# Reciprocals spread by fp16 matmuls, two steps moved to GpSimd, a third context piece, and new orders in a gated cross-attention block

## Chip, cores and metric

The kernel runs on one core of a Trainium2 chip. The metric is the device time of one execution in microseconds (us); lower is better. Of three runs the kernel before took 1135.02 us in the median (1132.27 to 1136.66).

## What is computed

x is 16 batches of 224 rows and 512 columns, the context 16 batches of 750 keys and 384 columns, with a mask over the keys; 8 heads of 64; the FFN has 2048 hidden columns.

```python
q = (layernorm(x) @ W_q);  k = context @ W_k;  v = context @ W_v      # split into 8 heads of 64
sim = einsum('bihd,bjhd->bhij', q, k) * 64 ** -0.5;  sim = where(mask, sim, -max)
x = x + tanh(g_xattn) * (softmax(sim) @ v @ W_o + b_o)
# bitlinear: rmsnorm the input, round it to 8 bits by its row's largest value; weights rounded to -1, 0, 1 by their mean
h = gelu(bitlinear(layernorm(x), w1, b1))
x = x + tanh(g_ffn) * bitlinear(h, w2, b2)
```

## The kernel before

Attention goes by batches: 16, each with two halves of 112 rows, 8 heads in 4 pairs, and so 16 score tiles of 112x750 (numbers u). The FFN goes by 28 tiles of 128 rows. Nearly every fp32 operand of the attention is split into an fp16 high part and an fp16 rest, and each product is three matmuls (high with high, rest with high, high with rest).

The order of the work is written out by hand as a list of steps, each named (kind, number), with a batch: START for the first batches, SLOTS for one round of a loop in which each step has a stage (which batch it works on relative to the round), and END. Every engine walks the same list and emits only its own part of a step, so the list fixes each engine's order; what engines wait for is said by semaphores (`need`). SP's queue (all loads, stores and transposes), GpSimd's and VectorE's are strictly in order.

The steps that matter here, with lines of the profile:

- LC loads one of three context pieces of a batch into one of two places (L482, it waits until GpSimd has used the piece two before). CX splits it: ScalarE makes the fp16 high part (L931), GpSimd the rest (L995). K and V need all three.
- LX loads x. N1 takes mean and variance on VectorE (L736, L740), and GpSimd raises the variance to the power -1/2 (L1008, L1011). XN subtracts the mean from x in place on VectorE (L744). XH scales and splits it (L925, L748), XT transposes it (L490), Q projects it.
- S makes two heads' scores of a half on TensorE (L574). M adds the mask and takes the row minimum on VectorE (L701), E exponentiates on ScalarE with a row sum (L881), H makes the fp16 high part on ScalarE (L888) or GpSimd (L979), L the rest on GpSimd (L984), T transposes both through SP (L507). There are five places for scores in SBUF, and M waits until L has freed one.
- R takes reciprocals of two row sums on VectorE (L708), 8 steps a batch. PV on TensorE first spreads the reciprocals of four (head, half) pairs over partitions by matmuls with the fp32 identity (L585, 112x64 stationary, 112 columns moving, fp32), then sums V weighted by the probabilities (L597, 36 matmuls of 224 columns). The two heads of a pair go side by side into the two halves of the array's columns. ScalarE copies the spread reciprocals out (L893) and VectorE multiplies (L713, step PA); PL splits the result (L899, L990).
- O is the output projection of a tile. L2 takes its statistics, subtracts the mean and finds the largest value, L3 derives the scale (L780 to L787), L4 multiplies and adds a large constant that rounds to an integer (L792) and subtracts it again (L797), both on VectorE. XQ transposes it, F1 is the first FFN product (L633), GE the gelu (L937), GS its sum of squares (L944), GM its largest value (L814), G2 the power and the scale (GpSimd L1038, L1041, then VectorE L821 to L828), GI the multiplication that rounds (GpSimd L1047), G3 the subtraction of the constant (VectorE L835), HT the transpose (L525), F2 the second product (L641) and the store.
- Weights are loaded and split once at the start (PD, PW), and the FFN's weights are rounded among the first two batches (WL, WA, WM, WB, WR, WQ).

## Time and profile before

| | |
|---|---|
| median of 3 runs | 1135.02 us |
| profiled execution | 1132.84 us |
| its span, first to last instruction | 1131.0 us |
| mean granted TensorE clock | 0.98 |
| busy: TensorE, VectorE, ScalarE, GpSimd | 91%, 80%, 70%, 76% |
| TensorE's weight loads (beside its matmuls) | 54% |

The profile is of one execution. A busy share is an average over stages with different limits, so the stretch has to be looked at. TensorE runs in pairs and pipelined: the time that a group occupies is read from the start of one group to the start of the next, rather than from its own busy time. "Waited for" names the engine and line whose work came last before an instruction could start.

### The profile page before, as it was taken

Reading aid. Unit: us, or ns where it says so; the run is one execution under the profiler, and the core shown is the slowest. Engines: PE = TensorE matmul, PEld = TensorE weight load, DVE = VectorE, ACT = ScalarE, POOL = GpSimd, SP = SyncE. Lnnn points to the kernel's source line nnn. Section 1 sums busy time; section 2 is a strip of 40 time slices with the busy share of each in tenths; the row PEclk is TensorE's granted clock in tenths of the full one; section 3 lists DMA queues with packets and bytes.
Section 4 is the critical chain, followed back from the end, with each engine's and each line's share of the span. In section 5 each row is a group of like instructions: output and inputs, shape, how many; then the busy total and the mean of one; then the engine's idle time right before and its main releaser. Section 6 shows DMA issues by size and latency. Waiting matters only on the chain.

```text
span 1131.0 us, 23832 instructions
## 1 busy us (share of the span) xinstructions
PE 1033.3 (91%) x8372; PEld 610.6 (54%) x8372; DVE 909.8 (80%) x1768; ACT 794.7 (70%) x1389; POOL 862.6 (76%) x767
## 2 busy tenths in 40 slices
PE   3869999999999899999999899999999999999575
PEld 2436556565555555565565555555565555655332
DVE  4678787979899587979989677998989778787764
ACT  4989685876868576786858668585967759586522
POOL 3389977787977778797877868788786879867832
PEclk9979999999999999999999999999999999999878
DMA  8778969777777977879687777868676896766822
GB/s 258 256 188 157 198 108 176 136 166 143 152 161 126 194 130 129 148 154 181 119 179 132 154 149 138 173 120 182 128 157 133 154 185 106 138 132 131 141 61 65
DMA packets 480005, 170.77 MB, mean 151 GB/s; under 512 B 458256, under 2 KB 460048, under 8 KB 479504
## 3 DMA queue, kind: packets, MB, share of 16 engines
q1 hardware_dynamic: 479888, 169.25, 74.6%
q8 instruction: 68, 1.11, 0.4%
q14 instruction: 49, 0.40, 0.1%
HBM read 48.09 MB, written 7.34 MB: 49 GB/s over the span
## 4 chain that ended last, share of the span: by engine, by line
PE 55%; POOL 16%; DVE 10%; issue 8%; DMA 6%; ACT 4%; SPq 1%; DVEq 0%; ACTq 0%; POOLq 0%
PE ps_g L544 29%; POOL p L984 8%; PE ps_g L641 7%; PE ps_g L597 6%; PE ps_s L574 6%; PE ps_g L633 5%; DMA hqt<-hq 4%; POOL p L979 2%; PE ps_g L585 2%; DVE prob L701 2%; DVE hq L835 1%; DVE xa L744 1%; ACT prob L881 1%; DMA xt<-xh 1%; POOL h_sb L1047 1%
## 5 line engine op out<-in xcount | busy, mean ns | idle before, releaser
L984 POOL TENSOR_TENSOR p<-prob,p 112x750 f16<-112x750 f32 x256 | 416.4, 1638 | 9.0 <-ACT p L888 4.9
L701 DVE CUSTOM_DVE_ANT_0 prob<-ps_s,mbias 112x750 f32<-112x750 f32 x256 | 235.6, 930 | 55.8 <-PE ps_s L574 52.9
L881 ACT ACTIVATE prob<-prob,rmin 112x750 f32<-112x750 f32 x256 | 233.6, 913 | 26.1 <-DVE rmin L701 25.8
L544 PE MATMUL ps_g<-ctx,wk 128*128 128x375 f16 x1152 | 203.2, 327 | 19.8 <-POOL ctx L995 18.1
L544 PE MATMUL ps_g<-wv,ctx 128*128 128x512 f16 (+1 forms) x864 | 204.0, 382 | 9.2 <-POOL ctx L995 6.2
L574 PE MATMUL ps_s<-k_sb,q_sb 64*112 64x375 f16 x1536 | 150.2, 328 | 17.0 <-DVE rmin L701 16.7
L544 PEld LDWEIGHTS ps_g<-ctx,wk 128*128 128x128 f16 x1152 | 108.3, 98 | 105.3 <-issue 35.5
L544 PEld LDWEIGHTS ps_g<-wv,ctx 128*128 128x128 f16 (+1 forms) x864 | 88.5, 104 | 96.5 <-issue 9.3
L888 ACT ACTIVATE p<-prob 112x750 f16<-112x750 f32 x160 | 129.5, 819 | 5.5 <-DMA pt<-p 4.6
L574 PEld LDWEIGHTS ps_s<-k_sb,q_sb 64*112 64x112 f16 x1536 | 90.5, 127 | 74.6 <-issue 41.9
L979 POOL CAST p<-prob 112x750 f16<-112x750 f32 x96 | 104.2, 1086 | 28.1 <-ACT prob L881 27.9
L641 PE MATMUL ps_g<-w,hqt 128*128 128x512 fp8e4 x432 | 100.5, 387 | 24.1 <-DMA hqt<-hq 24.1
L597 PE MATMUL ps_g<-pt,v_sb 128*64 128x224 f16 x2304 | 121.6, 259 | 0.2 <-DMA pt<-p 0.2
L597 PEld LDWEIGHTS ps_g<-pt,v_sb 128*64 128x64 f16 x2304 | 112.0, 110 | 0.4 <-issue 0.4
L633 PE MATMUL ps_g<-w,xqt 128*128 128x512 fp8e4 x432 | 102.0, 389 | 5.8 <-DMA xqt<-xq 5.6
L905 ACT ACTIVATE k_sb<-ps_g 128x375 f16<-128x375 f32 x128 | 61.1, 478 | 57.7 <-PE ps_g L544 56.9
L919 ACT ACTIVATE v_sb<-ps_g 128x512 f16<-128x512 f32 x96 | 56.5, 590 | 50.8 <-PE ps_g L544 50.8
L544 PE MATMUL ps_g<-xt,wq 128*128 128x224 f16 x768 | 85.5, 262 | 5.8 <-DMA xt<-xh 5.4
L893 ACT ACTIVATE rb<-ps_g 128x224 f32<-128x224 f32 x64 | 22.5, 351 | 92.5 <-PE ps_g L597 92.5
L995 POOL TENSOR_TENSOR ctx<-ctx_f,ctx 128x750 f16<-128x750 f32 x48 | 75.2, 1568 | 15.7 <-ACT ctx L931 14.8
L1047 POOL TENSOR_SCALAR h_sb<-h_sb,smh 128x2048 f32<-128x2048 f32 x27 | 53.3, 1974 | 41.3 <-DVE smh L828 41.3
L641 PEld LDWEIGHTS ps_g<-w,hqt 128*128 128x128 bf16 x432 | 42.1, 99 | 76.2 <-issue 30.6
(131 smaller groups left out, 1675.1 us busy)
## 6 DMA issues: line engine op xcount, KB each, us to landing
ctx_f<-in_ctx SPq DMA_DIRECT2D x48, 375.0 KB, 3.9
xa<-in_x SPq DMA_DIRECT2D x16, 448.0 KB, 4.8
xr<-in_x SPq DMA_DIRECT2D x28, 256.0 KB, 3.5
out<-xr SPq DMA_DIRECT2D x28, 256.0 KB, 2.3
pt<-p SPq DMA_TRANSPOSE x256, 3.9
h_sb<-in_w SPq DMA_DIRECT2D x4, 512.0 KB, 5.9
xr<-in_w SPq DMA_DIRECT2D x4, 512.0 KB, 6.7
pt<-in_w SPq DMA_DIRECT2D x3, 512.0 KB, 9.4
```

The source lines that it names most:

```text
L544: mm = nc.tensor.matmul(out, lhs, rhs, start=(m == 0), stop=(m == len(steps) - 1))
L574: mm = nc.tensor.matmul(ps_s[0:HT, e, c, 0:CH], q_sb[rows, j, qa, half * HT:(half + 1) * HT], k_sb[rows, j, ka, c * CH:(c + 1) * CH], star ...
L597: mm = nc.tensor.matmul(g[e * DH:(e + 1) * DH, 0:TQ] .rearrange("p (a q) -> p a q", a=2), v_sb[:, p, t, va, (2 * n + e) * DH:(2 * n + e + ...
L633: mm = nc.tensor.matmul(g[:, :], xqt_t[:, k, :], w1v[:, k, f * 512:(f + 1) * 512], start=(k == 0), stop=(k == KD - 1))
L641: mm = nc.tensor.matmul(g[:, :], hqt_t[:, k, :], w2v[:, k, :], start=(k == 0), stop=(k == KF - 1))
L701: nc.vector.tensor_tensor_reduce(prob[:, (b * NU + n) % PROBS, :].rearrange("p (c k) -> p c k", c=2), ps_s[0:HT, n % 2, :, 0:CH], mbias[:, ...
L881: nc.scalar.activation(prob[:, (b * NU + n) % PROBS, :], prob[:, (b * NU + n) % PROBS, :], ACT.Exp, bias=rmin[:, n:n + 1], scale=-1.0, acc ...
L888: nc.scalar.activation(p16[:, u % HILO, 0, 0:J], prob[:, (b * NU + n) % PROBS, :], ACT.Copy)\
L979: nc.gpsimd.tensor_copy(p16[:, u % HILO, 0, 0:J], prob[:, (b * NU + n) % PROBS, :]).then_inc(hi_pool, 1)
L984: nc.gpsimd.tensor_tensor(p16[:, u % HILO, 1, 0:J], prob[:, (b * NU + n) % PROBS, :], p16[:, u % HILO, 0, 0:J], ALU.subtract).then_inc(s[" ...
L995: nc.gpsimd.tensor_tensor(ctx[:, 1, n, :], ctx_f[:, (b * KC + n) % 2, :], ctx[:, 0, n, :], ALU.subtract)\
L1047: nc.gpsimd.tensor_scalar(h_t[:, :], h_t[:, :], smh[:, t % 2, 6:7], MAGIC, ALU.mult, ALU.add).then_inc(s["h_int"], 1)
```

## The change

1. **Reciprocals.** R now handles four at a time (4 steps a batch): after the reciprocal, VectorE makes an fp16 high part scaled by 1024 and, in a third instruction, the fp16 rest. Each waits for the one before. The identity is fp16 and holds 1/1024. PV spreads both parts with two accumulating fp16 matmuls in place of one fp32 matmul.
2. **Third context piece.** The third piece of the first batch has a place of its own (in the buffer of the transposed probabilities, not yet in use), so its load and that of the first piece of the next batch wait for less.
3. **XN** goes to GpSimd, as x times 1 plus the negated mean, after one small instruction that negates the means.
4. **The first half of L4** (multiply and add the constant) goes to GpSimd in the same form; VectorE then waits for it before the second half.
5. **Orders.** START, SLOTS, END and some stages are new. TensorE's order in the loop is nearly the same. At the start SP's queue was LC0, PD0, LC1, LM0, LX0, PD1, LC2 and becomes LC0, LC1, LX0, LM0, PD0, LC2, PD1; GpSimd's was MB, CX0, CX1, N1, CX2 and becomes N1, XN, CX0, CX1, MB, CX2; ScalarE's was PW0, CX0, CX1, XH0, XH1, CX2 and becomes CX0, XH0, XH1, CX1, CX2, PW0. For the last two tiles GpSimd's order was G2, GI, G2, GI and becomes G2, G2, GI, GI.

```diff
+RS = 1024.0
...
-        ident = sb("ident", [128, 128], F32)
+        ident = sb("ident", [128, 128], F16)
...
+        nm1 = sb("nm1", [HT, 2], F32)
...
+        rr16 = sb("rr16", [HT, 2, NU], F16)
...
+        def ctx_place(c):
+            return pt_words[:, 3 * WCH:3 * WCH + J] if c == KC - 1 else ctx_f[:, c % 2, :]
+
         def need_ctx(eng, c):
-            eng.wait_ge(d_ctx[c % 2], 16 * (c // 2 + 1))
+            if c == KC - 1:
+                eng.wait_ge(d_ctx[2], 16)
+            else:
+                eng.wait_ge(d_ctx[c % 2], 16 * (c // 2 + 1 - (c >= KC and c % 2 == 0)))
...
                     c = b * KC + n
-                    need(sp, "ctx_lo", 0, c - 2)
-                    sp.dma_start(ctx_f[:, c % 2, :], ctx_d[b, :, n, :]).then_inc(d_ctx[c % 2], 16)
+                    if c >= KC:
+                        need(sp, "ctx_lo", 0, c - 2 if c > KC + 1 else 1)
+                    sp.dma_start(ctx_place(c), ctx_d[b, :, n, :]).then_inc(d_ctx[2 if c == KC - 1 else c % 2], 16)
...
-                    need(pe, "recips", b, 2 * n + 1)
+                    need(pe, "recips", b, n)
                     for m in range(2 * n, 2 * n + 2):
                         at = 256 + half_of(b, m) * HT
-                        for e in range(2):
-                            nc.tensor.matmul(g[e * DH:(e + 1) * DH, at:at + HT],
-                                             rrec[:, 2 * m + e:2 * m + e + 1].to_broadcast([HT, DH]),
-                                             ident[0:HT, 0:HT], start=True, stop=True)
+                        for a in range(2):
+                            for e in range(2):
+                                nc.tensor.matmul(g[e * DH:(e + 1) * DH, at:at + HT],
+                                                 rr16[:, a, 2 * m + e:2 * m + e + 1].to_broadcast([HT, DH]),
+                                                 ident[0:HT, 0:HT], start=(a == 0), stop=(a == 1))
...
                 elif kind == "R":
-                    need(dve, "expd", b, 2 * n + 1)
-                    need(dve, "weighted", b - 1, n // 2)
-                    nc.vector.reciprocal(rrec[:, 2 * n:2 * n + 2], rsum[:, 2 * n:2 * n + 2])\
-                        .then_inc(s["recips"], 1)
+                    of = slice(4 * n, 4 * n + 4)
+                    need(dve, "expd", b, 4 * n + 3)
+                    need(dve, "weighted", b - 1, n)
+                    nc.vector.reciprocal(rrec[:, of], rsum[:, of]).then_inc(s["recips_f"], 1)
+                    need(dve, "recips_f", b, n)
+                    nc.vector.tensor_scalar(rr16[:, 0, of], rrec[:, of], RS, None, ALU.mult).then_inc(s["recips_hi"], 1)
+                    need(dve, "recips_hi", b, n)
+                    nc.vector.scalar_tensor_tensor(out=rr16[:, 1, of], in0=rrec[:, of], scalar=RS, in1=rr16[:, 0, of],
+                                                   op0=ALU.mult, op1=ALU.subtract).then_inc(s["recips"], 1)
...
-                elif kind == "XN":
-                    for half in range(2):
-                        need(dve, "x_mean", b, half)
-                        nc.vector.tensor_scalar(xa[:, half, :], xa[:, half, :], mv1[:, half, 0:1], None,
-                                                ALU.subtract).then_inc(s["x_cent"], 1)
...
-                    need_tile(dve, "x2_mult", t)
-                    nc.vector.tensor_scalar(xc[:, :], xc[:, :], sm2[:, t % 2, 6:7], MAGIC, ALU.mult, ALU.add)\
-                        .then_inc(s["x2_int"], 1)
...
+                elif kind == "XN":
+                    need(pool, "x_mean", b, 1)
+                    need(pool, "x_cent", b - 1, 1)
+                    nc.gpsimd.tensor_scalar(nm1[:, :], mv1[:, :, 0], -1.0, 0.0, ALU.mult, ALU.add)\
+                        .then_inc(s["x_less"], 1)
+                    need(pool, "x_less", b, 0)
+                    for half in range(2):
+                        nc.gpsimd.tensor_scalar(xa[:, half, :], xa[:, half, :], 1.0, nm1[:, half:half + 1],
+                                                ALU.mult, ALU.add).then_inc(s["x_cent"], 1)
+                elif kind == "L4":
+                    t = tile_of(b, n)
+                    need_tile(pool, "x2_mult", t)
+                    nc.gpsimd.tensor_scalar(xc[:, :], xc[:, :], sm2[:, t % 2, 6:7], MAGIC, ALU.mult, ALU.add)\
+                        .then_inc(s["x2_int"], 1)
```

The last line of END, with the old order of GI:0 and G2:1 (and F2:1 of batch 14) above and the new one below:

```diff
-    GM:1:-1 G3:0:-1 GI:0:-1 G2:1:-1 G3:1:-1 F2:0:-1 GI:1:-1 F2:1:-1
+    F1:4:-1 F1:5:-1 F1:6:-1 F1:7:-1 GM:0:-1 G2:0:-1 HT:0:-1 HT:1:-1 GS:1:-1 F2:1:-2 GM:1:-1 G2:1:-1 GI:0:-1 G3:0:-1
+    G3:1:-1 F2:0:-1 GI:1:-1 F2:1:-1
```

## Rows read from the trace of the kernel before

**Rows 1.** The page, part 1: busy us, share of the span, instructions.

```profile
PE 1033.3 (91%) x8372; PEld 610.6 (54%) x8372; DVE 909.8 (80%) x1768; ACT 794.7 (70%) x1389; POOL 862.6 (76%) x767
```

**Rows 2.** Busy us by stretch, with instruction counts, granted clock, DMA share and GB/s.

```profile
0.00:84.00 84.00, 51.81 (x310) 29.12 (x310) 52.06 (x94) 63.55 (x106) 45.37 (x44) 0.92 0.77 236
...
150.00:575.00 425.00, 415.11 (x3431) 247.38 (x3425) 361.34 (x710) 315.01 (x555) 346.79 (x307) 1.00 0.78 149
575.00:1000.00 425.00, 409.36 (x3355) 243.69 (x3357) 357.11 (x697) 302.62 (x534) 333.60 (x295) 1.00 0.76 147
```

**Rows 3.** TensorE's waits (us, times, longest): 150 to 1000, then 1000 to 1131.

```profile
PE ps_g L641 <- DMA hqt<-hq: 11.1, 7, 2.1
...
PE ps_s L574 <- DVE rmin L701: 10.3, 3, 5.8
```

**Rows 4.** Timeline of TensorE, 503 to 520: start, duration, line, operation, tiles, count.

```profile
503.50 0.60 PE L585 MATMUL ps_g<-ident,rrec 112*64 112x112 f32 x8
503.93 1.90 PE L597 MATMUL ps_g<-pt,v_sb 128*64 128x224 f16 x36
505.76 1.32 PE L544 MATMUL ps_g<-xt,wq 128*128 128x224 f16 x12
...
516.62 3.04 PE L544 MATMUL ps_g<-ctx,wk 128*128 128x375 f16 x18
519.49 0.81 PE L544 MATMUL ps_g<-wv,ctx 128*128 128x512 f16 x3
```

**Rows 5.** Groups by line and shape: count | busy us, mean ns | idle before.

```profile
L984 POOL TENSOR_TENSOR p<-prob,p 112x750 f16<-112x750 f32 x256 | 416.4, 1638 | 9.0 <-ACT p L888 4.9
...
L1047 POOL TENSOR_SCALAR h_sb<-h_sb,smh 128x2048 f32<-128x2048 f32 x27 | 53.3, 1974 | 41.3 <-DVE smh L828 41.3
...
L744 DVE TENSOR_SCALAR xa<-xa,mv 112x512 f32<-112x512 f32 x32 | 42.5, 1368 | 0.0
...
L792 DVE TENSOR_SCALAR xc<-xc,sm 128x512 f32<-128x512 f32 x28 | 30.8, 1098 | 0.1
...
L708 DVE RECIPROCAL rrec<-rsum 112x2 f32<-112x2 f32 x128 | 19.8, 156 | 23.4 <-ACT prob L881 23.2 <-issue 0.2
...
L770 DVE TENSOR_SCALAR xc<-xr,mv 128x512 f32<-128x512 f32 x28 | 14.1, 504 | 1.0
L1002 POOL TENSOR_SCALAR mbias<-mask 112x750 f32<-112x750 uint8 x16 | 13.8, 862 | 6.4 <-DMA mask<-in_mask 5.1
```

**Rows 6.** Timeline of all engines, 9 to 19.

```profile
10.61 1.29 DVE L736 BATCH_NORM_STATS2 st<-xa 112x6 f32<-112x512 f32 x2 [1.65 <-DMA xa<-in_x]
11.36 0.35 SPq L482 DMA_DIRECT2D ctx_f<-in_ctx  x1
...
12.98 0.25 POOL L1008 TENSOR_SCALAR ve<-mv 112x2 f32<-112x2 f32 x1
...
16.38 1.60 POOL L995 TENSOR_TENSOR ctx<-ctx_f,ctx 128x750 f16<-128x750 f32 x1 [2.23 <-ACT ctx L931]
...
18.14 1.10 PE L544 MATMUL ps_g<-ctx,wk 128*128 128x375 f16 x3 [18.14 <-POOL ctx L995]
```

**Rows 7.** Timeline of all engines, 1109 to 1124.

```profile
1110.11 1.97 POOL L1047 TENSOR_SCALAR h_sb<-h_sb,smh 128x2048 f32<-128x2048 f32 x1 [1.49 <-DVE smh L828]
...
1113.38 0.19 POOL L1038 TENSOR_SCALAR smh<-smh 128x1 f32<-128x1 f32 x1 [1.30 <-ACT k_sb L944]
1113.50 1.22 DVE L835 TENSOR_SCALAR hq<-h_sb 128x2048 bf16<-128x2048 f32 x1
1113.65 1.47 POOL L1041 TENSOR_TENSOR smh<-smh,half_neg 128x1 f32<-128x1 f32 x1
1114.74 1.96 SPq L525 DMA_TRANSPOSE hqt<-hq  x1
...
1119.13 5.16 PE L641 MATMUL ps_g<-w,hqt 128*128 128x512 fp8e4 x16 [9.28 <-DMA hqt<-hq]
```

## What the change should do to the time

> **What bounds the kernel now.** I read the share of busy time first, and stretch by stretch rather than as one average. TensorE is busy for 1033.3 of 1131.0 us [rows 1]. In the middle, from 150 to 1000 us, it is busy for 415.11 + 409.36 = 824.5 of 850 us [rows 2], so 25.5 us of idle time are left in 850, at a granted clock of 1.00, the 2.4 GHz level. In the same 850 us VectorE works 718.5 us (85%) and GpSimd 680.4 us (80%) [rows 2]. TensorE's largest single wait there is for the transposed FFN input, 11.1 us in seven places [rows 3]. So in the middle a TensorE microsecond taken away is nearly a microsecond of span, and work on the other engines counts only where it makes TensorE late. The rest of TensorE's idle time lies at the ends: 32.2 us in the first 84 us [rows 2], of which the first matmul's start is 18.14 us [rows 6], and the chain behind the last attention product.
>
> **The spread of the reciprocals (TensorE).** Each of the 64 PV steps begins with eight fp32 matmuls (L585: 4 products, each recorded as two) that spread the reciprocals over partitions. One such group starts at 503.50 and the weighted sum behind it at 503.93: 0.43 us of TensorE's time, though the row says 0.60, since the ends of matmuls overlap the next ones [rows 4]. The weighted sum itself, 36 fp16 matmuls of 224 columns in pairs, takes 505.76 - 503.93 = 1.83 us, 0.102 us for a pair [rows 4]. A pair of the fp32 ones takes 0.43 / 4 = 0.107 us with half the columns, 112. An fp32 column here costs as much as two fp16 columns. After the change there are still eight matmuls in four pairs, now fp16 with 112 columns. By columns: K's 18 matmuls of 375 columns take 519.49 - 516.62 = 2.87 us [rows 4], 0.159 us each, so 112 columns are 0.048 us, four pairs 0.19 us, and with about 0.05 us for the change-over 0.24 us. The gain is 0.43 - 0.24 = 0.19 us a group, 64 x 0.19 = **12.2 us**. Ends: nothing gained if a pair keeps its 0.107 us for a reason other than columns; at most 0.43 - 4 x 0.051 = 0.23 us a group, 14.5 us. I take 12.2, since every fp16 group in rows 4 goes by its columns.
>
> **The chain behind them (VectorE).** Before, a PV step needs two reciprocals of 0.156 us each, 128 in all, 19.8 us; after, one reciprocal of four columns, one scaling and one subtraction, each waiting for the one before. The two new ones are bounded by 0.15 and, with the wait, 0.25 us; the nearest row is the reciprocal itself, 0.156 [rows 5]. That is about 0.55 us x 64 = 35 us, 15 us more on VectorE. The PV step waits for the last exponential of the same four either way, and also for its transposes, which come behind a 1.64 us subtraction on GpSimd [rows 5], so the extra 0.3 us lies beside longer work: nothing. If that cover is gone, it is 0.3 x 64 = 19 us at most.
>
> **The mean of x and the scaling of the FFN input go to GpSimd.** VectorE loses 42.5 + 30.8 = 73.3 us [rows 5], and with the 15 above is 58 us lighter (80% to 75%). What I see in these rows is that the same subtraction on 128x512 costs 504 ns at L770, but L744 takes 1368 and L792 1098 ns: they are stretched by something beside them, and that goes too. GpSimd takes over 32 + 28 instructions of 512 columns. Its multiply-then-add takes 1974 ns for 2048 columns and 862 for 750 [rows 5]: 0.857 ns a column and 0.22 us fixed, so 0.66 us for 512. That is 60 x 0.66 = 39.6 us, and 16 negated means at 0.25 to 0.32 us (like the 0.25 of L1008 [rows 6]), 4.5 us: 44 us, 2.8 us for each of 16 batches (one takes about 67 us). GpSimd has 170 us idle in 850 [rows 2], 13 us a batch, so I cost it at nothing for TensorE, except as below. Queued behind the moved scaling on GpSimd are the subtractions that feed the transposes and free the score buffers; queued behind VectorE's second half of it are the next minimum and the evictions of K, V and Q that TensorE needs.
> At this place the Trainium skill speaks against the change: its GPSIMD Engine Reference, section "Engine selection", puts elementwise work on VectorE, with GpSimd about twice as slow for two inputs and near line rate for one. The trace agrees for the two-input subtraction and for one input shows 0.66 against 0.50 us unhindered; by the page as by the rows the moved work is a little longer where it goes.
>
> **Waits that take back part of it.** TensorE stands still in several places of a batch until something other than it comes [rows 3]; what is saved just before such a place only lengthens the wait. The bounds are none of the 12.2 us and half of it, or below nothing if the lighter VectorE shortens the waits (at most the 25.5 us of idle time, I allow 5). I take 2.0 us lost, about a sixth, since the idle time is 3% of the stretch and sits at about two places a batch, and there are four PV steps in one.
>
> **The start.** The first matmul waits until 18.14 us for the third context piece. Its load is issued at 11.36, behind GpSimd's work on the first piece, and its own subtraction on GpSimd runs from 16.38 to 18.0 [rows 6]. After the change it has a place of its own and is sixth in SP's queue without a wait; x comes third and wk fifth instead of second. x, fifth before, was there at 10.61 [rows 6] behind some 2.1 MB; with 1.2 MB ahead it lands at about 7.2 us, wk at 10.6 and the third piece at about 12. Then GpSimd's queue sets it: reciprocal deviation and centring of x until about 11.3, three subtractions of 1.6 and the mask's 0.9 us: 17.0 us. The split of wk (ScalarE 1.5, VectorE 1.8 us behind ScalarE's work on x and the pieces) ends at about the same time. So -1.1 us; bounds -3 and +1.5. The rest of the first 84 us is put in a new order with the same work; I cost it at nothing, bounds -5 and +5.
>
> **The end.** In the new order GpSimd does the root mean square of the last tile (G2) before the rounding multiplication of the last but one (GI), where it was the other way round. The last but one's product starts at 1110.11 and lasts 1.97 us, VectorE rounds at 1113.50 for 1.22 us, SP issues the transpose at 1114.74, and TensorE starts the product at 1119.13 [rows 7]. After, the multiplication stands behind the last tile's sum of squares, which GpSimd gets at 1113.38, and 0.19 us and a power: 1.47 us beside VectorE's rounding [rows 7], some 0.6 without it. So it runs from about 1114.2 to 1116.2, the rounding ends at 1117.5 instead of 1114.72, and the last 12 us come **2.8 us** later (bounds 1.5 and 4). Nothing hides this. The scaling of the two last tiles on GpSimd costs 0.66 for 0.5 us and two hand-overs, but in its new place it is not behind VectorE's read of the second output product: nothing, bounds -0.5 and +1.
>
> **The sum**, against the profiled execution's 1132.84 us: - 12.2 - 1.1 + 2.8 + 2.0 = 1124.3 us. That execution lies 2.2 us below the median of the three runs, 1135.02 (1132.27 to 1136.66); I add half of that and forecast **1125.5 us**.
>
> **The rivals.**
> (a) The fp16 pairs are paced by the instruction or its weight load, not by columns. Rows 4 have 36 matmuls with 36 loads in 1.83 us, 0.051 us for one with its load; if that is a fixed price, eight are 0.41 us and the gain is 0.02 x 64 = 1.3 us: 1132.84 - 1.3 - 1.1 + 2.8 = 1133.2, and 1134.4 with the offset. For it: no row shows an fp16 matmul under 224 columns. Against: each stage's time goes by its columns. If the price were higher for short ones, by 0.08 us each, a group would take 8 x 0.08 = 0.64 us, 0.21 more than now: + 13.4 - 1.1 + 2.8, 1148 us, slower. The 0.051 us of rows 4 speaks against it.
> The Trainium skill, TensorE: Matmul & The Clock Gate, section "Back-to-back issue gap", gives 81 ns for one load and matmul at 128 columns in a sustained stream, which is that higher price. Our row of 0.051 us at 224 columns is already below it.
> (b) Slower: GpSimd becomes late. The place is its queue: a scaling that waits for VectorE's multiplier holds the 1.64 us subtractions behind it, the transposes come late, score buffers are not freed, and TensorE waits in its score step, as it does now near the end of the loop for 10.3 us in three places, longest 5.8 [rows 3]. The price is the part of the added 44 us that comes on the path. It cancels the other terms' 8.5 us at a fifth, and makes the kernel slower by 0.5% from 15 us, a third. With half: 1124.3 + 22 = 1146 us. For it: 80% busy in the middle and 84% after, strictly in order. Against: VectorE's relief on the same chains, and 10 us a batch left idle.
> (c) The new orders, above all before 84 and after 1000 us, cost or give 5 to 10 us by themselves, in either direction: 1115 to 1135.
>
> **How the numbers follow.** The forecast's own mechanism, with a time between 1110 and 1129, has 0.60. Rival (a) has 0.12 as no change, and 0.03 as slower. Rival (b) has 0.13 as slower. Rival (c) has 0.12: 0.05 faster, 0.07 no change. A measurement of this kernel can tell about 0.5% from no change, so faster is below 1129.3, slower above 1140.7. That gives faster 0.65, same 0.19, slower 0.16. The range goes from 1132.84 - 14.5 - 3 - 5 = 1110 to 1140, which takes in (a) without change and small forms of (b), and leaves out half of (b) and the higher price of (a).
>
> **What would show it.** The next start behind the L585 line's successor at 0.24 us instead of 0.43; TensorE's idle time between 150 and 1000 us still about 30 us; GpSimd's busy time at about 907 us and VectorE's at about 850; the first matmul at 17 us; the wait before the last but one product some 12 us instead of 9.3 [rows 7]. The forecast is wrong if a group keeps 0.4 us, or if waits for the minimum (L701) or for transposes grow by over 10 us.

## The result, and the profile after

The changed kernel takes 1174.65 us in the median (1170.51 to 1176.19), the kernel before 1135.77 in runs on the same chip: a ratio of 1.0343, with an interval of 1.0307 to 1.0378. It is 3.4% slower, where 1125.5 us (1110 to 1140) was forecast. The profiled execution took 1175.45 us, its span is 1173.7 us, and the mean granted TensorE clock 0.97 instead of 0.98: TensorE was granted the 1.2 GHz level for 79.7 us of this span, where it was 44.4.

The page's part 1 of the changed kernel (busy us, share of the span, instructions), against [rows 1]:

```profile
PE 1031.4 (88%) x8372; PEld 602.1 (51%) x8372; DVE 953.9 (81%) x1772; ACT 796.3 (68%) x1389; POOL 892.5 (76%) x843
```

TensorE is busy for 2 us less. VectorE was given 73 us of work less, was expected at about 850 us, and has 953.9.

Busy us by stretch of the changed kernel (columns as in [rows 2]: the stretch and its length, then TensorE, its weight loads, VectorE, ScalarE and GpSimd, granted clock, DMA share, GB/s):

```profile
0.00:84.00 84.00, 40.91 (x242) 23.16 (x243) 48.77 (x68) 51.77 (x82) 44.20 (x44) 0.88 0.68 217
...
150.00:575.00 425.00, 398.34 (x3331) 235.14 (x3330) 364.03 (x692) 300.42 (x532) 339.30 (x329) 0.99 0.74 143
575.00:1000.00 425.00, 397.44 (x3297) 233.64 (x3294) 361.13 (x679) 302.54 (x529) 339.96 (x317) 0.99 0.76 146
```

Between 150 and 1000 us TensorE is busy for 795.8 us where it was 824.5 [rows 2]: its idle time has doubled, from 25.5 to 54.2 us in 850. In the first 84 us it does 11 us less work. To find where the span grew, I took the first score matmul (L574 before, L585 after) of each batch:

```
                          before    after
first scores, batch 0       29.6     34.4
first scores, batch 1       99.1    116.4
first scores, batch 15    1013.2   1057.4
end of the span           1131.0   1173.7
```

Of the 42.7 us of span, 17.3 are lost by batch 1 (4.8 of them ahead of batch 0), 26.9 in the next fourteen batches, and 1.5 come back behind batch 15.

What TensorE waited for in the changed kernel, whole span (us in total, times, longest):

```profile
PE ps_s L585 <- DVE rmin L713: 33.7, 16, 9.3
PE ps_g L653 <- DVE att L730: 25.4, 11, 2.7
PE ps_g L555 <- POOL ctx L1004: 23.0, 1, 23.0
PE ps_g L653 <- DMA hqt<-hq: 15.4, 6, 10.0
```

The same waits for VectorE in the kernel before, whole span (its L701 is the minimum, its L713 the step PA):

```profile
PE ps_s L574 <- DVE rmin L701: 16.7, 12, 5.8
PE ps_g L585 <- DVE att L713: 2.0, 1, 2.0
```

The multiplied attention output (L730, step PA) is late in eleven places for 25.4 us, where it was one place and 2.0 us. The wait for the row minimum (L713) has doubled; in the middle, from 150 to 1000 us, it went from 2.3 to 10.4 us. Both are VectorE's, and the minimum does not use the reciprocals at all. So I looked at what stands ahead of them in VectorE's queue.

Groups of the changed kernel by line and shape, columns as in [rows 5]:

```profile
L725 DVE SCALAR_TENSOR_TENSOR rr<-rrec,rr 112x4 f16<-112x4 f32 x64 | 64.6, 1010 | 2.2
...
L723 DVE TENSOR_SCALAR rr<-rrec 112x4 f16<-112x4 f32 x64 | 38.3, 599 | 2.2
...
L1029 POOL TENSOR_SCALAR xa<-xa,nm 112x512 f32<-112x512 f32 x32 | 22.1, 695 | 1.8
L1034 POOL TENSOR_SCALAR xc<-xc,sm 128x512 f32<-128x512 f32 x28 | 19.5, 695 | 0.9
...
L721 DVE RECIPROCAL rrec<-rsum 112x4 f32<-112x4 f32 x64 | 10.7, 167 | 0.0
```

The two small instructions of four columns cost 599 and 1010 ns on average. The reciprocal of the same four columns costs 167. Together R takes 64.6 + 38.3 + 10.7 = 113.6 us of VectorE's time; it took 19.8 before, and 35 were forecast. All 64 of one line at a time (min/median/max in ns, first and last start in us):

```profile
L725 DVE SCALAR_TENSOR_TENSOR rr<-rrec,rr x64: 161/1426/2531, 77.7 to 1111.7; 112x4 f16<-112x4 f32 x64
```

The same instruction takes 0.16 us at least and nine times that in the median. The timeline of all engines shows what it depends on. First at 500 us, then at 511 (start, duration, engine, line):

```profile
499.55 0.81 POOL L988 CAST p<-prob 112x750 f16<-112x750 f32 x1
...
500.01 0.37 DVE L723 TENSOR_SCALAR rr<-rrec 112x4 f16<-112x4 f32 x1
...
500.41 0.16 DVE L725 SCALAR_TENSOR_TENSOR rr<-rrec,rr 112x4 f16<-112x4 f32 x1
```

```profile
511.39 0.80 POOL L988 CAST p<-prob 112x750 f16<-112x750 f32 x1
...
511.54 0.17 DVE L721 RECIPROCAL rrec<-rsum 112x4 f32<-112x4 f32 x1
...
511.74 0.48 DVE L723 TENSOR_SCALAR rr<-rrec 112x4 f16<-112x4 f32 x1
512.16 3.08 POOL L993 TENSOR_TENSOR p<-prob,p 112x750 f16<-112x750 f32 x2
512.26 1.43 DVE L725 SCALAR_TENSOR_TENSOR rr<-rrec,rr 112x4 f16<-112x4 f32 x1
...
513.61 0.93 DVE L713 CUSTOM_DVE_ANT_0 prob<-ps_s,mbias 112x750 f32<-112x750 f32 x1
```

Each time, the end of the small instruction is the end of GpSimd's. The cast ends at 500.36 and the scaling at 500.38; at 511.39 + 0.80 = 512.19 the next cast ends, and the scaling at 512.22. The 3.08 us are two subtractions of half that; the first ends at about 513.7, and so does the rest (L725), at 513.69. The reciprocal at 511.54 runs beside the cast and takes no longer. At 500.41 GpSimd runs nothing, and the rest takes 0.16 us. Sorted by what GpSimd ran when it began, L725 took 161 to 165 ns in the 16 places where GpSimd was idle, and in the median 1521 ns in the 37 places beside a subtraction, ending 18 ns after it. Four times it began 0.09 us behind the start of GpSimd's 0.19 us step of two columns (L1025), and there it took 0.16 us: the price is what the instruction beside it has still to run. L723 beside one of GpSimd's steps with two inputs (45 places, 41 of them subtractions) took 649 ns in the median and ended 25 ns after it.

So these instructions have little work of their own; they stand still until GpSimd's running instruction is over, and the minimum (L713, at 513.61) and all that is queued in VectorE stands behind them. The Trainium skill states such a rule: SBUF — State Buffer, section "Who interferes with whom", says that VectorE and GpSimd share a pair of ports, that a two-input VectorE instruction or one in a two-port mode contends for it, and that whoever comes second is blocked for the whole of the other's instruction. The trace agrees, down to four columns, with the 18 and 25 ns above. Which mode the scaling (L723) runs in, no trace shows.

### The profile page after: what moved, and what is told of

The parts are those of the page before. It is cut to its first block, busy times and chain, and to the rows that moved or that the text cites. A ratio compares the mean times of both kernels' runs of the same rounds, so it can differ in the third digit from the quotient of the medians.

```text
span 1173.7 us, 23867 instructions
## 1 busy us (share of the span) xinstructions
PE 1031.4 (88%) x8372; PEld 602.1 (51%) x8372; DVE 953.9 (81%) x1772; ACT 796.3 (68%) x1389; POOL 892.5 (76%) x843
## 4 chain that ended last, share of the span: by engine, by line
PE 38%; DVE 25%; issue 15%; POOL 9%; DMA 7%; ACT 3%; SPq 1%; DVEq 0%; ACTq 0%; POOLq 0%
PE ps_g L555 18%; DVE prob L713 7%; PE ps_g L653 7%; PE ps_g L645 5%; PE ps_g L609 4%; PE ps_s L585 4%; POOL p L993 3%; DVE hq L844 3%; DMA hqt<-hq 2%; DVE smh L823 2%; DMA pt<-p 2%; DVE rr L723 2%; DVE h_sb L816 1%; DMA xqt<-xq 1%; DVE xh L760 1%
## 5 line engine op out<-in xcount | busy, mean ns | idle before, releaser
L713 DVE CUSTOM_DVE_ANT_0 prob<-ps_s,mbias 112x750 f32<-112x750 f32 x256 | 232.7, 930 | 45.6 <-PE ps_s L585 44.7
L890 ACT ACTIVATE prob<-prob,rmin 112x750 f32<-112x750 f32 x256 | 233.3, 912 | 17.3 <-DVE rmin L713 16.9
L555 PE MATMUL ps_g<-ctx,wk 128*128 128x375 f16 x1152 | 207.2, 326 | 24.5 <-POOL ctx L1004 23.0
L585 PE MATMUL ps_s<-k_sb,q_sb 64*112 64x375 f16 x1536 | 152.2, 331 | 34.1 <-DVE rmin L713 33.7
L653 PE MATMUL ps_g<-w,hqt 128*128 128x512 fp8e4 x432 | 106.7, 404 | 40.9 <-DVE att L730 25.4
L585 PEld LDWEIGHTS ps_s<-k_sb,q_sb 64*112 64x112 f16 x1536 | 91.2, 128 | 92.2 <-issue 46.8
L555 PEld LDWEIGHTS ps_g<-wv,ctx 128*128 128x128 f16 (+1 forms) x864 | 86.0, 103 | 99.1 <-issue 6.5
L609 PE MATMUL ps_g<-pt,v_sb 128*64 128x224 f16 x2304 | 124.4, 263 | 3.4 <-DMA pt<-p 3.4
L988 POOL CAST p<-prob 112x750 f16<-112x750 f32 x96 | 80.7, 841 | 43.1 <-ACT prob L890 33.3
L653 PEld LDWEIGHTS ps_g<-w,hqt 128*128 128x128 bf16 x432 | 42.7, 103 | 99.8 <-issue 31.9
L555 PE MATMUL ps_g<-wo,attn 128*128 128x512 f16 x336 | 79.8, 395 | 6.9 <-POOL attn L999 6.9
```

What stands on the lines that cost most here:

```text
L555: mm = nc.tensor.matmul(out, lhs, rhs, start=(m == 0), stop=(m == len(steps) - 1))
L585: mm = nc.tensor.matmul(ps_s[0:HT, e, c, 0:CH], q_sb[rows, j, qa, half * HT:(half + 1) * HT], k_sb[rows, j, ka, c * CH:(c + 1) * CH], star ...
L609: mm = nc.tensor.matmul(g[e * DH:(e + 1) * DH, 0:TQ] .rearrange("p (a q) -> p a q", a=2), v_sb[:, p, t, va, (2 * n + e) * DH:(2 * n + e + ...
L653: mm = nc.tensor.matmul(g[:, :], hqt_t[:, k, :], w2v[:, k, :], start=(k == 0), stop=(k == KF - 1))
L713: nc.vector.tensor_tensor_reduce(prob[:, (b * NU + n) % PROBS, :].rearrange("p (c k) -> p c k", c=2), ps_s[0:HT, n % 2, :, 0:CH], mbias[:, ...
L890: nc.scalar.activation(prob[:, (b * NU + n) % PROBS, :], prob[:, (b * NU + n) % PROBS, :], ACT.Exp, bias=rmin[:, n:n + 1], scale=-1.0, acc ...
```

## The experiments

New orders are those of the change, old orders those of the kernel before. Busy times are from the profile of each run. The kernel before took 1133.46, 1136.05, 1135.5 and 1135.33 us in the medians beside the four sets; the ratio is to it. e2, e9 and e11 to e15 leave out the fp16 rest of the reciprocals: their reciprocals have an fp16 high part alone, and their times only show what a part costs.

| kernel | us | ratio (interval) | VectorE busy |
|---|---|---|---|
| e1 new, fp32 spread | 1140.65 | 1.0044 (1.0016 to 1.0071) | 862.5 |
| e2 new, one fp16 reciprocal | 1131.7 | 0.998 (0.9955 to 1.0004) | 858.1 |
| e3 change in old orders | 1233.96 | 1.0886 (1.0828 to 1.0944) | 923.7 |
| e4 new orders alone | 1135.6 | 1.0011 (0.9983 to 1.004) | 882.8 |
| e5 old, fp16 pair alone | 1195.96 | 1.0511 (1.0451 to 1.0571) | 1008.2 |
| e6 new, pair by columns | 1139.41 | 1.0033 (1.0008 to 1.0057) | 901.4 |
| e7 e6 without the moves | 1141.43 | 1.0042 (1.0014 to 1.007) | 930.0 |
| e8 old, pair by columns | 1134.32 | 0.9993 (0.9975 to 1.0011) | 937.5 |
| e9 old, high part twice | 1131.71 | 0.9964 (0.9945 to 0.9983) | 907.7 |
| e10 e6, two exchanges | 1134.79 | 0.9995 (0.9976 to 1.0014) | 899.3 |
| e11 old, high part once | 1121.27 | 0.9868 (0.9846 to 0.989) | 911.6 |
| e12 new, once, exchanges | 1118.45 | 0.9853 (0.983 to 0.9875) | 860.5 |
| e13 e11 with the moves | 1153.78 | 1.0163 (1.0143 to 1.0183) | 826.6 |
| e14 e12, another start | 1115.97 | 0.9831 (0.9805 to 0.9857) | 854.2 |
| e15 e12 without the moves | 1117.27 | 0.9833 (0.9812 to 0.9853) | 892.9 |

### Which part costs it

The theory: the two small instructions hold VectorE's queue. The rivals: GpSimd late with the moved work, and the orders.

**e1.** The whole change, but with the reciprocals as before and spread in fp32:

```diff
-                        for a in range(2):
-                            for e in range(2):
-                                nc.tensor.matmul(g[e * DH:(e + 1) * DH, at:at + HT],
-                                                 rr16[:, a, 2 * m + e:2 * m + e + 1].to_broadcast([HT, DH]),
-                                                 ident[0:HT, 0:HT], start=(a == 0), stop=(a == 1))
+                        for e in range(2):
+                            nc.tensor.matmul(g[e * DH:(e + 1) * DH, at:at + HT],
+                                             rrec[:, 2 * m + e:2 * m + e + 1].to_broadcast([HT, DH]),
+                                             ident[0:HT, 0:HT], start=True, stop=True)
...
-                    nc.vector.tensor_scalar(rr16[:, 0, of], rrec[:, of], RS, None, ALU.mult).then_inc(s["recips_hi"], 1)
```

> The changed kernel with one part undone: reciprocals two at a time and the fp32 spread as before; the new orders, the moves to GpSimd and the third context piece stay. Theory A (the two new small instructions behind each reciprocal, 599 and 1010 ns in the changed kernel's profile, hold VectorE in front of the minima and evictions that TensorE needs): their 103 us go, TensorE gets back its 13 us for the fp32 spread, so 1140 to 1155 us. Theory B (GpSimd late through the moved steps) and theory C (the new orders are poorer by themselves): the time stays or rises by the fp32 spread, 1175 to 1188 us.

1140.65 us: 34.0 less than the changed kernel, with all orders and moves in place. GpSimd does the same work (892.6 us against 892.5), so its load is not the cause.

**e2.** The whole change, but R is one reciprocal that writes fp16, and this high part is spread twice, so TensorE's work is the change's:

```diff
-                    nc.vector.reciprocal(rrec[:, of], rsum[:, of]).then_inc(s["recips_f"], 1)
-                    need(dve, "recips_f", b, n)
-                    nc.vector.tensor_scalar(rr16[:, 0, of], rrec[:, of], RS, None, ALU.mult).then_inc(s["recips_hi"], 1)
-                    need(dve, "recips_hi", b, n)
-                    nc.vector.scalar_tensor_tensor(out=rr16[:, 1, of], in0=rrec[:, of], scalar=RS, in1=rr16[:, 0, of],
-                                                   op0=ALU.mult, op1=ALU.subtract).then_inc(s["recips"], 1)
+                    nc.vector.reciprocal(rr16[:, 0, of], rsum[:, of]).then_inc(s["recips"], 1)
```

> The changed kernel in which VectorE's step R is one reciprocal written straight as fp16; the two small instructions are gone, the fp16 rest of the reciprocals is left out and the high part is spread twice at half weight, so TensorE's work is the same as in the changed kernel. Theory A: VectorE falls from 954 to about 850 us and the time to 1130 to 1142 us. Theories B and C: within 6 us of 1174.7.

1131.7 us, 43.0 less than the changed kernel (41 by the ratios). The two small instructions are these 41 to 43 us. The result can be laid out in three steps, by the ratios: before to e1 + 5.0 us (orders, moves and the third context piece), e1 to e2 - 7.3 (the fp16 spread, with a cheap R), e2 to the change + 41.2. They add up to + 39 by their making, so the sum is no proof; the size of each step is what the runs show.

TensorE's work is the same in both kernels. The page of e2, part 1 (the changed kernel has 1031.4 us):

```profile
PE 1019.1 (90%) x8372; PEld 597.8 (53%) x8372; DVE 858.1 (76%) x1644; ACT 794.1 (70%) x1389; POOL 897.5 (80%) x843
```

The spans are 1173.7 and 1128.4 us. Of the 45.3 us between them TensorE is idle for 33 and busy for 12.3, with the same instructions. It is at 1.2 GHz for 79.7 us in the changed kernel and for 54.6 us in e2, and half of these 25.1 us is 12.5. So the stalls cost twice: some three quarters as waits, one quarter as a lower clock. The wait for the multiplied attention output is 0.7 us in e2 for 25.4; that for the minimum is 23.9 us for 33.7, so most of the latter does not come from the small instructions.

**e3.** All of the change in the old orders (the lists taken from the kernel before, with four R steps in the places of eight).

> All parts of the change but the orders: the old order lists with the steps R two by two merged into one at the place of the second. Theory A: the small instructions stall here too, 1160 to 1180 us. Theory C: 1125 to 1138 us, since only the orders were at fault. Theory B: 1160 to 1180 us as A, with longer waits for GpSimd.

**e4.** The code of the kernel before in the new orders.

> The kernel before with only the new order lists (each new step R gives the two old ones). Theory A and theory B: within 8 us of the kernel before, 1128 to 1144 us. Theory C: 1160 us or more.

e4 is no different from before. The four runs of e3 lie far apart, from 1217.03 to 1241.41 us (the ratio in the table is of all four), 42 to 67 us above the change; theory A had 1160 to 1180, so its size was missed. The new orders bring nothing to the old work, but in the old ones the new work costs more, in two ways. First the stalls reach the span more: in the middle of e3 TensorE waits 20.9 us for the rest of the reciprocals itself, a wait that hardly exists in the changed kernel (3.3 us, once). What TensorE waited for in e3, 150 to 1000 us:

```profile
PE ps_g L598 <- DVE rr L726: 20.9, 9, 2.4
PE ps_g L556 <- DVE att L731: 16.9, 7, 3.7
PE ps_g L598 <- DVE v_sb L735: 12.6, 9, 1.5
PE ps_g L556 <- DVE q_sb L746: 11.8, 9, 2.3
```

Second, VectorE waits in all 28 tiles for the half of L4 that went to GpSimd, where the changed kernel waits 13.5 us in 15 places:

```profile
DVE xq L807 <- POOL xc L1035: 115.1, 28, 6.0
```

What each is worth is in the runs below: the small instructions cost 62 to 64 us in the old orders (e5 against e9) and 41 to 43 in the new ones (the change against e2), and the moves cost 32.5 us in the old orders (e13).

### Is it the form of the instructions

**e5.** The kernel before with the fp16 pair alone: no moves, old orders, GpSimd's work as it was. Its edit is the reciprocals' part of the change's diff.

> The kernel before with only the reciprocals of the change (old orders, steps R merged two by two, x and the FFN input on VectorE, two context places). If the small instructions alone cause the loss, most of the 100 us of the previous old-orders run stays: 1185 to 1225 us. If the loss needs the moved work on GpSimd as well, 1125 to 1150 us.

1195.96 us, 5.1% or some 60 us more. Nothing else of the change is needed for the loss. VectorE has 98 us more than before. Its groups by line and shape:

```profile
L721 DVE SCALAR_TENSOR_TENSOR rr<-rrec,rr 112x4 f16<-112x4 f32 x64 | 63.3, 989 | 2.2
```

**e6.** The change with the same pair made in another form: the high part by a second reciprocal that writes fp16, the rest by four instructions of one column each, which take the fp32 value as a pointer operand; a second identity holds 1.

```diff
+                    nc.vector.reciprocal(rr16[:, 0, of], rsum[:, of]).then_inc(s["recips_hi"], 1)
...
-                    nc.vector.tensor_scalar(rr16[:, 0, of], rrec[:, of], RS, None, ALU.mult).then_inc(s["recips_hi"], 1)
...
-                    nc.vector.scalar_tensor_tensor(out=rr16[:, 1, of], in0=rrec[:, of], scalar=RS, in1=rr16[:, 0, of],
-                                                   op0=ALU.mult, op1=ALU.subtract).then_inc(s["recips"], 1)
+                    for u in range(4 * n, 4 * n + 4):
+                        lo = nc.vector.tensor_scalar(rr16[:, 1, u:u + 1], rr16[:, 0, u:u + 1], rrec[:, u:u + 1], -RS,
+                                                     ALU.subtract, ALU.mult)
+                    lo.then_inc(s["recips"], 1)
```

> The changed kernel with the same fp16 pair made without the two instructions that stall: a second reciprocal written as fp16 (0.17 us), and the rest by four one-column instructions with a pointer operand, which in the changed kernel never took over 0.215 us; the identity of the high part holds 1. Theory A (VectorE's instruction waits until GpSimd's two-input one ends): R costs about 1.0 us without a wait, 65 us in all instead of 114, and the time is 1135 to 1155 us. If instead any small fp16 result after a wait were slow, R stays above 1.5 us and the time near 1175 us.

1139.41 us, 35.2 less than the change, with three more instructions in each R. Groups of e6:

```profile
L728 DVE TENSOR_SCALAR rr<-rr,rrec 112x1 f16<-112x1 f16 x256 | 37.1, 209 | 7.6 <-DVE rr L724 0.9
...
L723 DVE RECIPROCAL rrec<-rsum 112x4 f32<-112x4 f32 x64 | 10.7, 167 | 0.0
L724 DVE RECIPROCAL rr<-rsum 112x4 f16<-112x4 f32 x64 | 9.3, 145 | 0.0
```

R is 57.1 us in six instructions where it was 113.6 in three. The longest of the 256 took 0.219 us, the longest reciprocal 0.174. None of these forms is held by GpSimd; number and dependency of the instructions cost far less than their form.

**e7.** e6 with XN and L4 back on VectorE.

> As the previous one, with x and the FFN input back on VectorE (new orders, third context place). Theory: the moves cost about 5 us where the small instructions are out of the way, as between the runs with the fp32 spread: 4 to 8 us faster than the previous run. Rival, the moves relieve VectorE: 5 to 10 us slower than it.

1141.43 against 1139.41 us, with overlapping intervals: the moves do nothing here that can be measured, and the 4 to 8 us expected were not there.

**e8.** The kernel before with the pair of e6, old orders, no moves.

> The kernel before with the fp16 spread alone, made without stalling instructions (old orders, merged steps R). If the fp16 spread's 12 us come through, 1122 to 1130 us; if VectorE's added 45 us in one piece before PV take them back, 1133 to 1150 us.

1134.32 us, no different from before. The fp16 spread does not pay for its own R even in this form.

### What the fp16 spread is worth

**e9.** The kernel before with one fp16 reciprocal per four and the high part spread twice (the edit of e2 in the old kernel).

> The kernel before with the fp16 spread and VectorE's R as one reciprocal of four columns written as fp16; the fp16 rest of the reciprocals is left out and the high part spread twice at half weight. TensorE saves the forecast's 12 us and VectorE 11 us. If a TensorE microsecond is nearly a microsecond of span, 1121 to 1126 us; if the next wait takes it (the second FFN product's transposed input, which waited 25 us instead of 11 in the middle once columns were used), 1127 to 1134 us.

Start to start, a spread group takes 0.220 us in the median of the 64, where it took 0.433: 64 x 0.213 = 13.6 us of TensorE's time. The kernel gains 0.36%, some 4 us. Part of the missing 10 is in the waits from 150 to 1000 us: for the FFN input 13.0 us instead of 11.1, for the minimum 6.5 instead of 2.3; with other waits that fell, TensorE's idle time there goes from 25.5 to 30.4 us. Part is the clock. TensorE is at 1.2 GHz for 58.0 us of this span, against 44.4 before, and half of the 13.6 us more is time lost, 6.8 us. The granted clocks of all runs bear it out: by them (twice the share of the clock that is missing, times the span) the ten runs of e9 are at 1.2 GHz for 54.7 us on average, the 21 of the kernel before for 45.3. One such place, TensorE's timeline of e9:

```profile
374.29 5.30 PE L650 MATMUL ps_g<-w,hqt 128*128 128x512 fp8e4 x16 [2.13 <-DMA hqt<-hq]
```

Behind a wait of 2.13 us these 16 matmuls take 5.30 us, at the 1.2 GHz level; in most other places the same 16 take 3.62 us. Time saved just ahead of a wait lengthens the wait. The three stretches at 1.2 GHz in the middle of e9 each come right behind such a wait (2.13, 2.07 and 1.98 us); but a wait of 2.11 us in e9 and one of 2.08 us in the kernel before were followed by none, so it is not shown that the added length made the clock fall. Idle time and clock come to 11.7 us, against the 10 that are missing; each kernel has one profile only, so they say where the gain went and not how it is shared out.

**e11.** e9 with the high part spread once, so four matmuls for eight:

```diff
-                        for a in range(2):
-                            for e in range(2):
-                                nc.tensor.matmul(g[e * DH:(e + 1) * DH, at:at + HT],
-                                                 rr16[:, 0, 2 * m + e:2 * m + e + 1].to_broadcast([HT, DH]),
-                                                 ident[0:HT, 0:HT], start=(a == 0), stop=(a == 1))
+                        for e in range(2):
+                            nc.tensor.matmul(g[e * DH:(e + 1) * DH, at:at + HT],
+                                             rr16[:, 0, 2 * m + e:2 * m + e + 1].to_broadcast([HT, DH]),
+                                             ident[0:HT, 0:HT], start=True, stop=True)
```

> As e9, with the high part spread once: two pairs of matmuls a step instead of four, so the rest of the reciprocals is left out and TensorE saves another 64 x 0.10 = 6 us. If TensorE still sets the time, 4 to 6 us below e9, 1116 to 1122 us; if its waits do, within 2 us of e9.

A group takes 0.122 us, 64 x 0.311 = 19.9 us less than before, and the kernel is 14.2 us faster. The time at 1.2 GHz is 44.4 us, as before, and the wait for the FFN input falls to 7.0 us. So 6 us more on TensorE gave 10 us more of span than e9, where 4 to 6 were expected; the clock (13.6 us less at 1.2 GHz, half of it time) and that wait go in this direction.

### The ends, and the moves

**e10.** e6 with the third context piece's split ahead of the mask at the start, and GI:0 ahead of G2:1 at the end:

```diff
-    LC:0:0 N1:0:0 XN:0:0 CX:0:0 XH:0:0 XH:1:0 CX:1:0 MB:0:0 CX:2:0 PW:0:0 PW:1:0 N1:0:1 LC:1:0 XN:0:1 WB:0:0 QL:0:0
+    LC:0:0 N1:0:0 XN:0:0 CX:0:0 XH:0:0 XH:1:0 CX:1:0 CX:2:0 MB:0:0 PW:0:0 PW:1:0 N1:0:1 LC:1:0 XN:0:1 WB:0:0 QL:0:0
...
-    F1:4:-1 F1:5:-1 F1:6:-1 F1:7:-1 GM:0:-1 G2:0:-1 HT:0:-1 HT:1:-1 GS:1:-1 F2:1:-2 GM:1:-1 G2:1:-1 GI:0:-1 G3:0:-1
+    F1:4:-1 F1:5:-1 F1:6:-1 F1:7:-1 GM:0:-1 G2:0:-1 HT:0:-1 HT:1:-1 GS:1:-1 F2:1:-2 GM:1:-1 G3:0:-1 GI:0:-1 G2:1:-1
```

> The run with new orders, columns and moves (1139.4 us), with two pairs of steps in the order lists exchanged: at the start GpSimd's mask step behind its third context piece (it took 5.02 us there beside VectorE's split of wk and wq), and for the last tiles GpSimd's GI of the last but one before G2 of the last. First matmul from about 22 to 18 us and the end 2 to 3 us sooner: 5 to 8 us faster, 1132 to 1135 us. If the start's 4 us only lengthen a later wait, 2 to 3 us faster.

4.6 us less than e6 for both, with ratios whose intervals just overlap; 5 to 8 us were expected. From batch 15's first scores to the end e10 takes 113.0 us and e6 116.3, so 3.3 us of it are at the end. At the end the wait of the last but one product falls to 8.87 us, about the 9.28 of [rows 7]. At the start little is won: the first matmul comes at 21.32 us. The timeline of all engines of e10:

```profile
15.25 5.92 POOL L1008 TENSOR_TENSOR ctx<-pt,ctx 128x750 f16<-128x750 f32 x1
```

Now the context step is the one that stands still, 5.92 us for a step of 1.60 [rows 6], beside VectorE's splits of wk and wq. What runs on GpSimd at that time is held, whichever it is.

**e12.** e10 with the high part once, by one fp16 reciprocal.

> New orders and moves with the high part spread once (the fp16 rest is left out) and the two exchanges of e10: the run with the high part spread twice (1131.7 us) less 6 us for TensorE and 5 to 8 us for the ends, 1117 to 1122 us.

1118.45 us; against e11 the ratios' intervals overlap, so new orders, moves and exchanges together are no better than the old kernel with the same edit.

**e13.** e11 with XN and L4 on GpSimd, in the old orders; the edit is that part of the change's diff.

> e11 (old orders, high part spread once, the fp16 rest left out) with the subtraction of the mean and the first half of L4 on GpSimd. If the moves relieve the loop, 3 to 8 us faster than e11's 1121.3; if VectorE's wait for GpSimd in the old place of L4 costs more, 3 to 15 us slower, with new waits of VectorE for GpSimd's xc.

32.5 us more than e11, where 3 to 15 were expected of this mechanism. VectorE's waits:

```profile
DVE xq L797 <- POOL xc L1025: 116.4, 28, 5.5
```

All 28 tiles: VectorE reaches the second half of the scaling before GpSimd has made the first, and stands for 4.2 us on average, with the evictions behind it. TensorE then waits for those:

```profile
PE ps_g L593 <- DVE v_sb L725: 13.9, 10, 1.5
PE ps_g L552 <- DVE q_sb L736: 11.1, 9, 1.8
```

In the changed kernel the first of these waits is 13.5 us in 15 places. The new orders put more between the two halves.

**e14.** e12 with wk and all three context pieces loaded and split ahead of x.

```diff
-    LC:0:0 N1:0:0 XN:0:0 CX:0:0 XH:0:0 XH:1:0 CX:1:0 CX:2:0 MB:0:0 PW:0:0 PW:1:0 N1:0:1 LC:1:0 XN:0:1 WB:0:0 QL:0:0
-    K:0:0 K:1:0 KL:0:0 KL:1:0 K:2:0 LX:0:0 KL:2:0 LM:0:0 PD:0:0 Q:0:0 PW:2:0 WA:0:0 K:3:0 XH:0:1 M:0:0 S:0:0 LC:2:0
+    LC:0:0 PD:0:0 LC:1:0 LC:2:0 CX:0:0 PW:0:0 CX:1:0 CX:2:0 MB:0:0 N1:0:0 XN:0:0 XH:0:0 XH:1:0 PW:1:0 N1:0:1 XN:0:1 WB:0:0 QL:0:0
+    K:0:0 K:1:0 KL:0:0 KL:1:0 K:2:0 LX:0:0 KL:2:0 LM:0:0 Q:0:0 PW:2:0 WA:0:0 K:3:0 XH:0:1 M:0:0 S:0:0
```

> e12 (new orders, moves, high part once, the rest left out) with another start: SP loads the first context piece, wk, the second and the third piece, then x; ScalarE and VectorE split wk before x; GpSimd takes the three pieces before x. The first matmul comes at 12 to 14 us instead of 20.8. If its lateness is what the start loses, the time falls by 3 to 8 us to 1111 to 1115 us; if the scores of the first batch wait for x and the order behind it, it stays within 2 us of 1118.5 or rises.

1115.97 us, the lowest median here, though its interval overlaps those of e12 and e15; 1111 to 1115 was expected. TensorE's timeline of e14:

```profile
12.18 6.09 PE L556 MATMUL ps_g<-ctx,wk 128*128 128x375 f16 x27 [12.18 <-POOL ctx L999]
...
23.32 2.40 PE L556 MATMUL ps_g<-xt,wq 128*128 128x224 f16 x12 [5.04 <-DMA xt<-xh]
```

The first matmul comes 8.6 us sooner than in e12 (20.75), yet the first scores only 0.7 us sooner (30.0 against 30.7), since Q now waits for x. The date of the first matmul is not what the start costs.

**e15.** e12 with the moves undone.

> e12 with the subtraction of the mean and the first half of L4 back on VectorE (the fp16 rest of the reciprocals is left out). If the moves are worth something in their own orders, 3 to 10 us slower than e12's 1118.5; if they only shift work, within 3 us.

1117.27 against 1118.45 us, overlapping intervals. The moves are worth nothing in the new orders and cost 32.5 us in the old ones (e13).

## Why the prediction was wrong

**The spread** was right and a little small: 0.22 us a group (forecast 0.24), here in the changed kernel's timeline of TensorE:

```profile
501.91 0.39 PE L597 MATMUL ps_g<-ident,rr 112*64 112x112 f16 x8
502.13 1.89 PE L609 MATMUL ps_g<-pt,v_sb 128*64 128x224 f16 x36
```

Rival (a) falls with it: eight matmuls with their loads in 0.22 us are 0.028 us each, below the 0.051 that it took as a fixed price. The 81 ns that the Trainium skill gives for 128 columns (TensorE: Matmul & The Clock Gate, "Back-to-back issue gap") do not hold for these matmuls of 112 columns, which go in pairs into the two halves of the array's columns; the measurement decides.

**The chain behind them** is the step that failed, the term "0.15 and, with the wait, 0.25 us" for each new instruction. They measured 0.60 and 1.01 us. The row it was taken from, the reciprocal's, is one of a form that GpSimd does not hold (167 ns beside everything). The prediction had the right rows in hand in its next paragraph: the same subtraction at 504 and at 1368 ns, "stretched by something beside them" [rows 5]. It counted this as time that goes away with the moved work, and did not ask whether the two added instructions would be stretched too. With GpSimd busy for 80% of the middle, and for about half of that in subtractions of 1638 ns [rows 5], an instruction that waits out the running one comes to somewhere between 0.15 and 1.6 us. For 128 instructions the upper bound was thus some 205 us of VectorE's time and not 32. Nor did the stretching go away with the moved work: VectorE's total came out some 100 us above the forecast's, 79 of them in R, and the second half of L4 and the rest of x, which stayed on VectorE, each took 7 to 8 us more than before (39.0 for 31.6, 48.2 for 40.5).

The second half of that step, that the delay "lies beside longer work: nothing", failed as well. It looked only at who needs the reciprocals. PV hardly waits for them (3.3 us, once), but VectorE's queue is in order, and what waits is what stands behind: the minimum and PA. Against e2, which has the same orders and moves, the wait for PA grew from 0.7 to 25.4 us and that for the minimum from 23.9 to 33.7. The prediction's own sign, waits for the minimum up by over 10 us, did come: they went from 16.7 to 33.7 us, though 23.9 are there in e2 without the small instructions. The bound "if that cover is gone, 19 us at most" was made with the same 0.3 us and fell with it. Undoing the form (e6) took back 35 us, undoing the instructions (e2) 41 to 43. What the prediction had no term for is the clock, a quarter of that.

**The moves**, costed at nothing, were worth nothing (e15, e7). GpSimd's instruction measured 0.695 us, forecast 0.66; its busy time is 892.5 us, forecast 907. That rival (b) was bound to the orders was not seen: in the old ones its mechanism costs 32.5 us (e13), through VectorE's wait for the first half of the scaling rather than through late score buffers.

**The start.** Forecast 17 us for the first matmul, measured 23.04. The timeline of all engines of the changed kernel:

```profile
12.61 4.04 DVE L760 SCALAR_TENSOR_TENSOR xh<-xa,rs,xh 112x512 f16<-112x512 f32 x2 [2.96 <-ACT xh L934]
...
16.18 5.02 POOL L1011 TENSOR_SCALAR mbias<-mask 112x750 f32<-112x750 uint8 x1
16.57 1.74 DVE L670 SCALAR_TENSOR_TENSOR wk<-xr,wk 128x1536 f16<-128x1536 f32 x1
...
18.23 2.28 DVE L670 SCALAR_TENSOR_TENSOR wq<-h_sb,wq 128x2048 f16<-128x2048 f32 x1
...
21.29 1.61 POOL L1004 TENSOR_TENSOR ctx<-pt,ctx 128x750 f16<-128x750 f32 x1
...
23.04 1.41 PE L555 MATMUL ps_g<-ctx,wk 128*128 128x375 f16 x4 [23.04 <-POOL ctx L1004]
```

It is the same effect with the engines exchanged. The mask step, costed at 0.9 us, begins beside VectorE's rest of x (L760) and stands for 5.02 us, until the two splits of weights behind that are through as well (20.51), all three with two inputs; the third context piece is behind it. That explains 4 of the 6 us. The term "the rest of the first 84 us: nothing, -5 to +5" was too narrow: from batch 0 to batch 1 the change takes 82.0 us where it was 69.5. The orders alone take 74.7 there (e4), so some 5 us are of the new START list. With it TensorE waits 15.5 us for minima between 34 and 116 us (e4; longest 8.1), where it was 3.8 before, and a wait of 6.2 us for a context piece is gone. The other 7 us are open. e2, with the cheap R, takes 74.4, which would put them on the small instructions; but e6, where those do not stall, takes 81.1, e15 81.2 and e7 85.1.

**The end.** Forecast was a wait of 12 us for the last but one product, measured 10.0. The timeline of all engines of the changed kernel:

```profile
1152.50 0.19 POOL L1061 TENSOR_SCALAR smh<-smh 128x1 f32<-128x1 f32 x1 [3.02 <-ACT k_sb L953]
1152.77 0.56 POOL L1064 TENSOR_TENSOR smh<-smh,half_neg 128x1 f32<-128x1 f32 x1
1153.32 1.97 POOL L1070 TENSOR_SCALAR h_sb<-h_sb,smh 128x2048 f32<-128x2048 f32 x1
...
1161.02 5.87 PE L653 MATMUL ps_g<-w,hqt 128*128 128x512 fp8e4 x16 [10.00 <-DMA hqt<-hq]
```

The term was right. With the orders alone (e4) and in e2 the longest wait of this kind is 12.2 and 12.3 us. In the changed kernel, from the last tile's sum of squares on GpSimd to the product it is 1161.02 - 1152.50 = 8.5 us, and it was 1119.13 - 1113.38 = 5.75 [rows 7], 2.8 more as forecast. Yet that sum of squares itself comes 2 us sooner behind TensorE's last work than before, since ScalarE's gelu of the last tile no longer waits 1.63 us for VectorE. The forecast took the date of this step over from the old order. From batch 15's first scores to the end the change is even 1.5 us shorter than before (116.3 against 117.8).

**Waits that take back part of it** (+2.0): the wait for the FFN input did shrink, but in e9, where little else is changed, 10 of 13.6 us were taken back. That term was also far too small, and so was its bound, "half of it". These 10 us did not decide the sign, since e2, with the whole gain of the spread and nothing of the stalls, came out where the kernel before is.

The direction was missed as well. The rivals for slower were a higher price of short matmuls and a late GpSimd. Neither came, so the 0.16 given to slower was for other mechanisms than the one that made it so.

## What to carry to other kernels

Price a small VectorE instruction by its form and by what GpSimd runs, not by its size: with two SBUF inputs, or as a scaling of several columns, it costs the rest of GpSimd's current instruction, and everything queued behind it pays; reciprocals and one-column forms did not wait. When a row of a profile shows the same shape at two durations, find out what stretches it before adding instructions of that kind. Count a wait of TensorE with the clock that follows it: here a quarter of the loss was work done at the lower level. And where an in-order queue gets a new instruction, look at who stands behind it, not only at who needs its result.

## What the runs showed of the hardware

- A VectorE instruction of four columns takes 0.16 us with GpSimd idle and up to 2.53 us otherwise; in the median of those beside a subtraction it is 1.52. Beside the same work a reciprocal of four columns stays at 0.160 to 0.174 us, one that writes fp16 averages 0.145 and a one-column scaling with a pointer operand 0.209.
- It goes both ways: GpSimd's mask step took 5.02 us beside VectorE's two-input splits, and 0.83 in the median of its 16, and a context split 5.92 for 1.60 (e10). VectorE's three such instructions in a row did not let it in between.
- An fp16 matmul of 112 columns with its load, in pairs in the two halves of the array's columns, takes 0.028 us.
- The same TensorE instructions were busy for 12.3 us more in the changed kernel than in e2, with 25.1 us more at the 1.2 GHz level.
- Less TensorE work can come with a lower clock: in e9 the time at 1.2 GHz rose by 13.6 us when 13.6 us of work was taken out, and in e11, with 6 us more taken out, it was back at 44.4. Why it came back is open.
